# Graph-network edge stage: each row gather also waits for TensorE's relation rows of the same tile, two groups back

## What is computed

```python
def _mgcn_conv(x, edge_index, edge_type, rel, W_in, W_out, W_loop, b, n):
    src, dst = (edge_index[0], edge_index[1])
    half = e // 2
    m = x[src] * rel[edge_type]
    m = jnp.concatenate([m[:half] @ W_in, m[half:] @ W_out], 0)
    ...
    agg = jax.ops.segment_sum(m * norm[dst][:, None], dst, num_segments=n)
    return jnp.tanh(agg + x @ W_loop + b)
```

## Time and profile before

| what | us |
|---|---|
| median of 3 runs | 3587.01 (3585.84 to 3588.12) |
| the profiled execution's own time | 3595.48 |
| its span, first to last instruction | 3593.7 |
| PE busy | 3030.8 (84%) |
| DVE busy | 2375.1 (66%) |
| POOL busy | 1927.0 (54%) |
| ACT busy | 1851.9 (52%) |
| mean granted TensorE clock | 0.917 |

### The profile page before, as it was taken

How to read it: one execution, slowest core, us unless ns; L and a number is a source line. 1 busy time by engine, 2 the same in 40 slices (tenths; PEclk the granted TensorE clock), 3 DMA queues, 4 the chain that set the end, 5 groups by cost and what they waited for, 6 DMA issues and landing times. The chain is left out here.

```text
span 3593.7 us, 61044 instructions
## 1 busy us (share of the span) xinstructions
PE 3030.8 (84%) x21236; PEld 2804.9 (78%) x21236; DVE 2375.1 (66%) x3620; ACT 1851.9 (52%) x3333; POOL 1927.0 (54%) x2028
## 2 busy tenths in 40 slices
PE   3788888888888888796988888888888887776998
PEld 1688888888788888696887777788887786776998
DVE  5566666666666666794666666666666666996666
ACT  5455555555555555484555555555555554444443
POOL 3655555555555555355555555555555553774332
PEclk9898999899989898897899999988999988998999
DMA  7222222222222222243222222222222222332222
GB/s 233 86 80 82 80 80 83 79 81 79 81 81 79 81 81 80 70 163 95 78 81 81 81 81 81 81 79 80 80 80 81 81 81 70 109 114 91 71 70 67
DMA packets 163452, 313.57 MB, mean 87 GB/s; under 512 B 34381, under 2 KB 96269, under 8 KB 163189
## 3 DMA queue, kind: packets, MB, share of 16 engines
q0 software_dynamic: 79872, 218.21, 21.1%
q1 hardware_dynamic: 82389, 91.10, 7.9%
q10 hardware_dynamic: 928, 0.85, 0.1%
HBM read 264.16 MB, written 45.88 MB: 86 GB/s over the span
## 5 line engine op out<-in xcount | busy, mean ns | idle before, releaser
L606 PE MATMUL edge_rg<-edge_rel_hi,edge_hot 128*128 128x256 f32 x6656 | 1654.7, 306 | 93.4 <-issue 76.7
L606 PE MATMUL edge_rg<-edge_rel_lo,edge_hot 128*128 128x256 f32 x4992 | 1405.4, 305 | 42.6 <-issue 40.7
L606 PEld LDWEIGHTS edge_rg<-edge_rel_hi,edge_hot 128*128 128x128 f32 x6656 | 1321.5, 213 | 137.6 <-issue 129.6
L450 ACT ACTIVATE edge_hot<-edge_typ,minus_type 128x512 fp32r<-128x512 f32 x832 | 527.1, 685 | 1331.1 <-PE edge_typ L595 648.4
L606 PEld LDWEIGHTS edge_rg<-edge_rel_lo,edge_hot 128*128 128x128 f32 x4992 | 1066.0, 214 | 87.3 <-issue 72.5
L424 POOL DMA_INDIRECT edge_xg<-h,src x832 | 787.5, 947 | 591.1 <-DVE edge_rg L502 354.8
L424 POOL DMA_INDIRECT edge_xg<-emb,src x832 | 788.7, 948 | 586.3 <-DVE edge_rg L502 338.9
L502 DVE TENSOR_TENSOR edge_rg<-edge_xg,edge_rg 128x1024 f32<-128x1024 f32 x416 | 509.7, 1225 | 678.7 <-remote 569.1
L493 DVE TENSOR_SCALAR edge_hot<-edge_typ,type_of 128x512 fp32r<-128x512 f32 x832 | 584.5, 743 | 184.7 <-ACT edge_hot L450 117.2
L508 DVE TENSOR_TENSOR edge_m_lo<-edge_rg,edge_m_hi 128x1024 fp32r<-128x1024 f32 x416 | 504.1, 1212 | 2.3 <-ACT edge_m_hi L442 2.3
L456 ACT ACTIVATE edge_hot<-edge_hot 128x512 fp32r<-128x512 f32 x832 | 484.0, 639 | 0.0
(11 more groups left out here) (160 smaller groups left out, 3946.9 us busy)
## 6 DMA issues: line engine op xcount, KB each, us to landing
edge_xg<-emb,src POOLq DMA_INDIRECT x832
edge_xg<-h,src POOLq DMA_INDIRECT x832
set_x_rows<-in_x SPq DMA_DIRECT2D x25, 256.0 KB, 3.7
emb<-set_e_rows SPq DMA_DIRECT2D x25, 256.0 KB, 3.5
emb_t<-set_e_t SPq DMA_DIRECT2D x25, 256.0 KB, 3.0
dense_prev<-emb_t SPq DMA_DIRECT2D x25, 256.0 KB, 2.8
h_t<-dense_work SPq DMA_DIRECT2D x25, 256.0 KB, 2.0
h<-dense_work SPq DMA_DIRECT2D x25, 256.0 KB, 2.2
```

Of the source, the lines that this page charges most:

```text
L450: act.activation(hot[:, q % 2, c], typ[q % 2][:], ACT.Abs, bias=K["minus_type"][:, c:c + 1]).then_inc(distances, 1)
L606: ins = pe.matmul(rg[q % 2][:, t, :], hot[:, q % 2, c, t * P:(t + 1) * P], part[:, c, :], start=(c == 0 and part is rel_hi), stop=(c == FULL))
```

## The change

A new semaphore `rel_tile` counts the first three tiles of `relation_rows` of each group; the fourth is counted by `rel_done`, as before. The gather of tile t of group g now waits for tile t of `relation_rows` of group g-2 as well as, at the head of the group, for `messages` of g-4. Nothing else differs. (`wait_past` leaves out a wait for a value of 0 or less, so the first groups wait for less.)

```diff
         rel_done = s.sem("rel_done")
+        rel_tile = s.sem("rel_tile")
...
                 wait_past(pool, messages, g + 1 - GROUPS_IN_RING)
                 for t in range(GROUP):
+
+                    if t < GROUP - 1:
+                        wait_past(pool, rel_tile, (GROUP - 1) * (g - 2) + t + 1)
+                    else:
+                        wait_past(pool, rel_done, g - 1)
                     at = K["src"][:, GROUP * g + t:GROUP * g + t + 1]
                     pool.indirect_dma_start(xg[:, GROUP * q + t, :], None, nodes,
...
                             ins = pe.matmul(rg[q % 2][:, t, :], hot[:, q % 2, c, t * P:(t + 1) * P], part[:, c, :],
                                             start=(c == 0 and part is rel_hi), stop=(c == FULL))
+                    if t < GROUP - 1:
+                        ins.then_inc(rel_tile, 1)
                 ins.then_inc(rel_done, 1)
```

## The result

| | before | after |
|---|---|---|
| median, us | 3586.43 (3584.93 to 3588.12, 4 runs) | 3428.28 (3422.88 to 3432.6, 4 runs) |
| the profiled execution's own time | 3595.48 | 3432.17 |
| its span | 3593.7 | 3430.4 |
| mean granted TensorE clock | 0.917 | 0.946 |

The ratio is 0.9558, 95% interval 0.954 to 0.9576: 158 us faster, where 207 were forecast (3380).

The account below looks back on a forecast made before the run. Gather streams holding PE's semaphore updates were taken to bound the edge stages at 6.59 us a group. Increments, waits and later gathers 0, restart -229, extra stops +20 gave -209 us: forecast 3380 us, range 3140 to 3660.

Parts of the forecast that it names:

- The diagnosis: Edge stages: PE's semaphore updates, late in a gather stream, wait until it has landed; some 1.15 us lost a group.
- first rival: Edge stages: pacing cures the hold, PE bounds at 5.44 us a group; 3109 us if full, 3100 to 3270; chance 0.17.
- Increments: PE, relation matmuls: three more semaphore increments a group, 1248 in all, cost 0.
- The bound of 150 us: PE, relation matmuls: upper cost if each of 1248 increments took one 0.12 us matmul slot.
- Waits on POOL: POOL, ahead of gathers: four waits a group cost 0; at most 0.02 to 0.1 us each.
- Later gathers hidden: Edge-stage gathers: issued some 5 us later, need 6.7 us against 10.9 of cover, 4 us to spare; cost 0.
- The restart: POOL between streams: restarts without the message, idle 2.05 instead of 3.06 us; 229 us less, 20 back for extra stops.
- the count stays near 227: POOL's stops: POOL and PE balance near seven gathers a stream, 6.0 us a group, so the number of stops holds.
- Signs: Profile after: POOL's idle about 450 us in 220 to 250 stops, DVE's wait under 400, messages 6.0 to 6.2 apart.
- slower rival: POOL's new gate: its own reports are held by the stream, 400 stops of 2 us, mostly 3600 to 3700; chance 0.25.

Follow-up runs that it names:

- whole-group gate: Kernel before plus one wait at each group's head for all relation rows of g-2: 3540.05 us, ratio 0.9863 (holding chip); 2933.89 us, ratio 1.001 (free chip).
- the gate a group earlier: Changed kernel waiting on relation tiles of g-3 instead of g-2: 2931.59, 2930.87 and 2931.6 us on chips where the kernel before takes about 2931.

## Why the prediction came out as it did

**The diagnosis was right.** The gather stream holds PE's reports, and this was what the kernel lost its time to. The price is read now: 3592.24 - 2952.94 = 639 us with all gathers but the first 16 of each stage gone, on the same chip. I had put the loss at 1.15 us a group, 416 x 1.15 = 478 us.

The traces also have the times of most semaphore updates, and with them the hold can be read straight, where the prediction had only what came after it. The table pairs each update in the two edge stages with the latest earlier instruction that raises that semaphore (semaphores that one engine alone raises there):

| kernel, chip | PE: updates over 1 us late | longest, us | DVE, ACT: longest, us |
|---|---|---|---|
| before, holding | 677 of 1364 | 9.7 | 0.01 |
| changed, holding | 583 of 1158 | 6.5 | 0.01 |
| no gathers, holding | 3 of 1436 | 6.7 | 0.01 |
| increments alone, free | 0 of 1233 | 0.02 | 0.01 |

It is PE's updates alone that are late; none of VectorE or ScalarE is.

**Why it was 1.15 and should have been 1.54.** I took 5.44 us for PE's free turn. It is 5.05, in the changed kernel's first turn (851.52 - 846.47) as well as with no gathers and on a free chip. The 5.44 was a turn that already held small delays, by the hold as I read it. 6.59 - 5.05 = 1.54 us, and 416 x 1.54 = 641, which agrees with the 639 measured. So the first rival's floor was also wrong: a full cure would give about 3587 - 641 = 2946 us, not 3109. No edit that keeps the gathers came near it on a holding chip.

**Increments (taken as 0): right.** Alone they gave 1.0004, and the upper end of the interval, 0.14% of 2931, is 4 us. In the changed kernel a tile's last matmul and the one after it stay 0.12 us apart; they stand in one row, "x2":

```profile
847.40 0.28 PE L612 MATMUL edge_rg<-edge_rel_lo,edge_hot 128*128 128x256 f32 x1
847.52 0.40 PE L612 MATMUL edge_rg<-edge_rel_hi,edge_hot 128*128 128x256 f32 x2
847.76 0.28 PE L612 MATMUL edge_rg<-edge_rel_lo,edge_hot 128*128 128x256 f32 x1
```

The bound of 150 us is out. The Trainium skill (TensorE: Matmul & The Clock Gate, "The cost: per-tile semaphore tail") would give 1248 x 26.3 ns = 33 us on the path, an estimate; the measured interval, of a free chip, excludes that for increments in the middle of a run of matmuls.

**Waits on POOL (0): right.** The gap at a wait already met is 0.30 to 0.31 us (852.07, 857.75), and on three free chips a kernel with the four waits took the same time as the one without (ratios 1.0001, 1.0 and 1.0).

**Later gathers hidden: right for this gate.** No wait ahead of the message is put down to a gather's transfer (L508: remote 172 times, PE 71, issue 4). The whole-group gate, a little later for tiles 0 to 2, did uncover them on a free chip (78.9 us), so the cover is thinner in the second stage than my 4 us to spare.

**The restart: here a step failed.** For a held stop I forecast 3.0 us from last issue to next gather and 2.05 idle; the row shows 3.06 and 2.12. But I took this as the size of every stop, kept their number near 227, and gave 20 us for some 20 more. There were 409, of 1664 / 409 = 4.1 gathers each, and they are 1.34 us on average. POOL's idle time in these rows fell by 693.7 - 547.0 = 147 us where the sum had 229 - 20 = 209. (All its idle time ahead of gathers, with the stops booked as "issue", fell by 166 us, from 1177.4 to 1011.1; 20 us of this went into the gathers themselves, which took 961 and 958 ns in the two stages in place of 948 and 947. No term had that, and its cause is open.) The 62 us between forecast and measurement of this term account for the 49 by which the time was missed, within the rough match of POOL's idle time to the span.

The step that failed is "the count stays near 227", and behind it the picture of the new gate. The balance of POOL and PE near seven gathers a stream took streams as ending only when POOL had caught up with its gate, and breaks inside a group as rare and due to a late tile. In fact the reports of the tiles are held like those of the groups, and each can stop POOL: in 359 of 422 stops the tile was done before POOL asked for it. The gate took the hold over, in more and shorter stops. Nor does a hold always last until the stream has ended, as I had read from the kernel before: 83 of 176 held messages of the changed kernel start while the gathers go on. That short streams are what lets more of PE's reports through in time is my reading of the stretch above, supported by the whole-group gate's smaller gain but not isolated by a run. So the nearness of the total is in part luck: I had 227 x 2.05 + 20 = 485 us of POOL's stops and 547 were measured, where the number had been set too low by 40% (247 for 409) and the size too high by half (2.05 for 1.34).

**Signs.** POOL's stops name PE L612: yes. Its idle falls to about 450: it was 547. DVE's unexplained wait under 400: 343.7. Messages 6.0 to 6.2 us apart: 6.18, and 6.26 in the first stage, just outside. The stops: 409 of 1.34 us, not 220 to 250 of 2 us. The first rival's many short stops came about in part (409, some under 1 us), without its cure, since streams of four still meet a hold. The slower rival's mechanism, a gate whose own reports are held, came about in most stops; its price did not, as the stops are not 2 us each but 1.34. The clock rose from 0.917 to 0.946; that this is because PE stalls less was not shown, and the whole-group gate was faster than the kernel before at a lower clock (0.906 to 0.909 beside 0.918 to 0.940).

**What stays open.** Why a chip holds or not; whether descriptors or bytes do it; how the saving depends on the gate's distance; and the changed kernel's time on a free chip, which was not taken. The nearest there, its increments alone and the gate a group earlier, both changed nothing. No version that beats the changed kernel on a holding chip was found.

## What to carry to other kernels

When an engine waits and the trace names no one, look for what else runs and ends at a fixed distance before the wait's end, and test it by taking that work out. When a trace does name an engine, compare the end of that engine's instruction with the moment the waiting one was free: here it had been done in most cases. Pace background transfers by the progress of the critical engine, in units as small as the transfers, rather than letting them run as far ahead as the buffer allows; a coarser gate kept a third of the gain. This was tried on a chip that holds; on the others there was nothing to gain. Time the kernel before on the chip at hand before ascribing anything: here the same program took 2931 or 3592 us.

## What the runs showed of the hardware that was not expected

- Two kinds of chip for one program: 3584.7 and 3592.2 us on two chips, 2930.6 to 2932.2 on five, with granted clocks of 0.918 to 0.940 and 0.975 to 0.981 in runs of the kernel before. Each chip was visited in one sitting, so a property of the chip cannot be told from a state that it was in then. The difference, 653 to 662 us, is the hold and nearly nothing else: without gathers beyond the first 16 of each stage a holding chip takes 2953, and 21.3 us of that are the two holds in these 16.
- On a holding chip it is PE's semaphore updates that come late while gathers run, over 1 us in 677 of 1364; no update of VectorE or ScalarE came more than 0.02 us after its instruction in the same trace.
- In the kernel before, the held messages start 2.84 us (median of 185) after the stream's last issue, after a wait of up to 4.9 us. In the changed kernel, where streams are short, 83 of 176 start while the stream still runs, and the longest wait is 5.7 us (L508 above).
- On a free chip 1664 gathers in unbroken streams cost the kernel no measurable time (2930.55 with, 2931.11 without all but 32 of them).
- 1248 more semaphore increments on TensorE in mid-stream cost about 4 us together at most, on a free chip.
